# Layer 3's expert outputs: rows of X with bias and weight gathered by slot, sums scattered straight into the output

## The reference

```python
def _L3_ffn_ref(x, W1, b1, Wg, bg, Wd, bd):
    xf = x.reshape(-1, orig_shape[-1])                  # 625 x 256, layer-normed
    H = jax.nn.gelu(xf @ W1 + b1, approximate=False)    # 625 x 1024
    probs = jax.nn.softmax((H @ Wg + bg) / TEMP, axis=-1)
    assign = jnp.argmax(probs, axis=-1)
    out = jnp.zeros_like(xf)
    for e in range(Wd.shape[0]):                        # 8 experts
        y = H @ Wd[e] + bd[e]                           # 1024 -> 256
        sel = (assign == e)[:, None]
        out = out + jnp.where(sel, probs[:, e:e + 1] * y, 0.0)
    return out.reshape(orig_shape)
...
    x = x + _L3_ffn_ref(_layernorm(x, axis=-1)[None], ...)[0]
    return x
```

## Time and profile before

| what | us |
|---|---|
| median of three runs | 972.86 (970.52 to 976.18) |
| the profiled execution, its own time | 975.67 |
| its span, from first to last instruction | 973.5 |
| PE busy in the span | 892.7 (92%) |
| DVE busy | 447.8 (46%) |
| ACT busy | 281.1 (29%) |
| POOL busy | 182.1 (19%) |

### The profile page before, as it was taken

The page is one execution under the profiler, slowest core; times in us unless marked ns, Lnnn a source line. Parts: engine busy times, 40 slices in busy tenths (PEclk is TensorE's granted clock), DMA queues, the critical chain, the costliest instruction groups (busy, mean ns, idle before and its releaser), DMA issues.

```text
span 973.5 us, 15475 instructions
## 1 busy us (share of the span) xinstructions
PE 892.7 (92%) x5638; PEld 710.7 (73%) x5638; DVE 447.8 (46%) x1433; ACT 281.1 (29%) x625; POOL 182.1 (19%) x177
## 2 busy tenths in 40 slices
PE   6999998999999999999996778999999999899897
PEld 4776656889999877889875667777887554665665
DVE  7988555522222421632278976423434142340623
ACT  5111263122222114233347853332111111114210
POOL 2201000122221200045427751000101100000231
PEclk9999899999999999899988979999998899799899
DMA  8303001288885603159241000353100000320696
GB/s 296 142 2 92 1 1 38 96 303 315 320 325 192 235 1 130 54 187 322 98 164 68 1 1 1 130 192 120 45 1 14 19 1 1 130 96 35 206 344 230
DMA packets 28007, 120.42 MB, mean 124 GB/s; under 512 B 5401, under 2 KB 10032, under 8 KB 20132
## 3 DMA queue, kind: packets, MB, share of 16 engines
q1 hardware_dynamic: 22362, 104.39, 30.1%
q0 software_dynamic: 5280, 14.95, 4.6%
q10 hardware_dynamic: 295, 0.14, 0.1%
HBM read 106.11 MB, written 13.36 MB: 123 GB/s over the span
## 4 chain that ended last, share of the span: by engine, by line
PE 71%; DVE 15%; DMA 5%; issue 5%; ACT 2%; DVEq 1%; POOL 1%; SPq 0%; POOLq 0%; ACTq 0%
PE PS L817 8%; PE PS L473 6%; PE PS L441 5%; PE PS L832 5%; PE PS L884 4%; PE PS L868 4%; PE PS L485 4%; PE PS L552 4%; PE PS L627 2%; PE PS L908 2%; PE PS L959 2%; PE PS L948 2%; PE PS L1268 2%; DMA HT<-flat_rows,route 2%; DVE ring L1991 2%
## 5 line engine op out<-in xcount | busy, mean ns | idle before, releaser
L441 PE MATMUL PS<-const 128*128 128x128 f32 x674 | 92.8, 299 | 5.8 <-DVE X L1358 2.1
L441 PEld LDWEIGHTS PS<-const 128*128 128x128 f32 x674 | 88.2, 212 | 10.2 <-DVE X L1358 2.9
L817 PE MATMUL PS<-HT,ring 128*128 128x128 f32 x680 | 79.1, 275 | 3.3 <-DVE HT L1512 1.7
L817 PEld LDWEIGHTS PS<-HT,ring 128*128 128x128 f32 x680 | 78.4, 192 | 4.6 <-issue 3.9
L2655 POOL TENSOR_TENSOR col<-col,power 125x4 f32<-125x4 f32 (+2 forms) x13 | 11.9, 917 | 315.4 <-DVE col L1351 226.5
L2715 POOL DMA_INDIRECT slot_rows<-ST,route x41 | 41.4, 1010 | 151.1 <-ACT ST L2429 96.0
L2753 POOL TENSOR_TENSOR arena<-arena,ring 125x625 f32<-125x625 f32 x40 | 55.7, 1416 | 34.3 <-ACT arena L2517 30.1
L1911 DVE TENSOR_TENSOR HT<-HT,PS 128x256 f32<-128x256 f32 (+1 forms) x51 | 19.1, 376 | 89.8 <-ACT HT L2418 71.6
L627 PE MATMUL PS<-HT 125*128 125x126 bf16 x530 | 41.7, 230 | 6.8 <-DVE HT L1722 6.7
L1049 PE MATMUL PS<-w,HT 125*64 125x125 f32 x400 | 30.3, 305 | 18.0 <-DVE w L2010 18.0
L832 PE MATMUL PS<-ring,HT 128*128 128x256 f32 x204 | 46.8, 380 | 0.0
(11 more groups left out here) (472 smaller groups left out, 1712.3 us busy)
## 6 DMA issues: line engine op xcount, KB each, us to landing
ring<-in_experts SPq DMA_DIRECT2D x17, 1386.0 KB
ring<-in_experts SPq DMA_DIRECT2D x17, 768.0 KB, 6.0
ring<-in_experts SPq DMA_DIRECT2D x11, 1026.0 KB
arena<-in_experts SPq DMA_DIRECT2D x10, 1024.0 KB
ring<-in_experts SPq DMA_DIRECT2D x7, 1024.0 KB, 7.6
arena<-in_experts SPq DMA_DIRECT2D x6, 1026.0 KB
arena<-in_gnn SPq DMA_DIRECT2D x5, 1024.0 KB, 5.9
ring<-in_experts SPq DMA_DIRECT2D x8, 513.0 KB, 3.7
```

The source lines that it names most:

```text
L441: pe.matmul(PS[:, bank, 0:128], ident, ident, start=True, stop=True)
L817: mm = pe.matmul(PS[:, bank, at:at + SLOTS], both[:, j, k, m * 128:(m + 1) * 128], xs[0][i % 2][:, k, :], start=(k == 0), stop=(k == KD - 1))
```

## The change

Layer 3 no longer scatters to a cleared buffer, reads back and mixes. DVE writes the sum of X and the weighted bias rows to `X_weight` (257 columns a token, the last one the token's weight, with one more small copy), SP writes it to HBM as `weighted_rows` (640 KB, 1028 bytes a row), and POOL gathers those rows by slot as it gathers the hidden rows (`gather_start`, four ahead, nine in all). When a block's product is ready, DVE computes `PSUM * weight + row` in one operation (two for the last block), and POOL scatters the 128 rows (64 in the last block) into the output itself. Numbers of free slots lie over the bound of 624. Blocks 7 and 8 go the same way as the others, so the one-hot matrices and `add_late` fall away, and so do the read back, `mix_rows(3)`, the writes of X and the clearing in layer 0.

```diff
-SENT = {L: BLOCKS[L] - {3: 2}.get(L, 0) for L in PICKS}
@@ routing(L), DVE
+                row, less = dest_, float(pairs)
+                if L == 3:
+                    row, less = table[:, 0:blocks], 1.0
+                    link(dve.scalar_tensor_tensor(row, table[:, blocks:2 * blocks], float(TP), row, ALU.mult, ALU.add))
+                dve.scalar_tensor_tensor(to_row[:, 0:blocks], row, -less, empty_, ALU.add, ALU.add).then_inc(rows_ready, 1)
@@ layer0_moe(), DVE
-                dve.wait_ge(copy_out, 64)
@@ layer3_moe(), PE
-                for i in range(SENT[3], BLOCKS[3]):
-                    add_late(i)
@@ layer3_moe(), DVE
                 for t in range(NT):
                     b = bank()
-                    taken(dve.tensor_tensor(X[:, t, :], X[:, t, :], PS[0:TP, b, 0:D], ALU.add))
+                    taken(dve.tensor_tensor(X_weight[:, t, 0:D], X[:, t, :], PS[0:TP, b, 0:D], ALU.add))
                 own_banks()
-                token = CONST(const, "iota")[:, 0:N].rearrange("q (p t) -> q t p", t=NT)
-                for j in range(BLOCKS[3] - SENT[3]):
-                    dve.tensor_scalar(late_hot[j], token, float(NT), dest[:, SENT[3] + j:SENT[3] + j + 1], ALU.add,
-                                      ALU.is_equal).then_inc(picks_ready, 1)
+                dve.tensor_copy(X_weight[:, :, D:D + 1], mixes(3)).then_inc(layer_done, 1)
...
                         dve.wait_ge(ys_full, BASE[3] + i)
-                        if i > AHEAD[3]:
-                            dve.wait_ge(ys_out[b], rounds(3, i - 1 - AHEAD[3]))
-                        if i < BLOCKS[3]:
-                            dve.tensor_copy(ys[3][:, b, :], PS[:, 5 + (i - 1) % 2, 0:D]).then_inc(ys_taken, 1)
-                        else:
+                        dve.wait_ge(rows_moved[b], rounds(3, i - 1) - 16)
+                        parts = 64 if i == BLOCKS[3] else 128
+                        start = slot_start[0:parts, b, :]
+                        ins = dve.scalar_tensor_tensor(ys[3][0:parts, b, :], PS[0:parts, 5 + (i - 1) % 2, 0:D], start[:, D:D + 1],
+                                                       start[:, 0:D], ALU.mult, ALU.add)
+                        if i == BLOCKS[3]:
+                            link(ins)
                             dve.wait_ge(left_taken, BLOCKS[3] + 1)
-                            dve.tensor_tensor(ys[3][0:64, b, :], PS[0:64, 5 + (i - 1) % 2, 0:D], upper_half,
-                                              ALU.add).then_inc(ys_taken, 1)
-                mix_rows(3)
...
+                            ins = dve.scalar_tensor_tensor(ys[3][0:64, b, :], upper_half, start[:, D:D + 1], ys[3][0:64, b, :],
+                                                           ALU.mult, ALU.add)
+                        ins.then_inc(ys_taken, 1)
@@ exchange(L), POOL
             def scatter(L, i):
                 b = i % AHEAD[L]
                 pool.wait_ge(ys_taken, BASE[L] + i + 1)
+                if L == 3:
+                    parts = 64 if i == BLOCKS[3] - 1 else 128
+                    pool.indirect_dma_start(final, bass.IndirectOffsetOnAxis(to_row[0:parts, i:i + 1], 0),
+                                            ys[3][0:parts, b, :], None, bounds_check=N - 1,
+                                            oob_is_err=False).then_inc(rows_moved[b], 16)
+                    return
...
+            def gather_start(i):
+                b = i % AHEAD[3]
+                pool.indirect_dma_start(slot_start[:, b, :], None, weighted_rows,
+                                        bass.IndirectOffsetOnAxis(from_row[:, i:i + 1], 0),
+                                        bounds_check=N - 1, oob_is_err=False).then_inc(rows_moved[b], 16)
...
                 pool.wait_ge(rows_ready, 2 * NTH[L] + 2)
+                if L == 3:
+                    pool.wait_ge(copy_out, 64)
+                    for i in range(AHEAD[3]):
+                        gather_start(i)
                 for i in range(BLOCKS[L]):
                     if i + AHEAD[L] < BLOCKS[L]:
                         gather(L, i + AHEAD[L])
-                    if i < SENT[L]:
-                        scatter(L, i)
+                    scatter(L, i)
+                    if L == 3 and i + AHEAD[3] < BLOCKS[3]:
+                        gather_start(i + AHEAD[3])
@@ SP
-            sp.wait_ge(xn_ready, 2 * NT)
-            cleared = slot_rows[3][0:N, :].rearrange("(p t) d -> p t d", t=NT)
-            for p0, p1 in ((0, 120), (120, TP)):
-                sp.dma_start(cleared[p0:p1], nothing[p0:p1].unsqueeze(1).broadcast_to([p1 - p0, NT, D])).then_inc(copy_out, 16)
...
+            sp.wait_ge(layer_done, 1)
+            for p0, p1 in ((0, 120), (120, TP)):
+                sp.dma_start(weighted_rows.rearrange("(p t) d -> p t d", t=NT)[p0:p1], X_weight[p0:p1]).then_inc(copy_out, 16)
             sp.wait_ge(spill_ready, NTH[3] + 1)
...
-            rows_back(3)
-            for t in range(NT):
-                sp.wait_ge(layer_done, NT + t + 1)
-                sp.dma_start(out[0:120, t, :], X[0:120, t, :]).then_inc(out_done, 16)
-            sp.wait_ge(out_done, 160)
+            for b in range(AHEAD[3]):
+                sp.wait_ge(rows_moved[b], rounds(3, max(range(b, BLOCKS[3], AHEAD[3]))))
```

More of the change, by code:

```diff
@@ L66, in rounds @@
     b = i % AHEAD[L]
-    earlier = sum(len(range(b, SENT[M], AHEAD[M])) for M in PICKS if M < L and b < AHEAD[M])
-    return 16 * (earlier + i // AHEAD[L] + 1)
+    earlier = sum(len(range(b, BLOCKS[M], AHEAD[M])) for M in PICKS if M < L and b < AHEAD[M])
+    return 16 * (earlier + (2 if L == 3 else 1) * (i // AHEAD[L] + 1))
 def arrived(L, i):
@@ L350, in build @@
         mixed = {L: spare[0:TP, 0:2 * NT * D].rearrange("p (t k d) -> p t k d", t=NT, k=2) for L in (0, 1)}
-        mixed[3] = ROOT[:, :, :].unsqueeze(2)
         xs_rows = {0: view(spare, 2 * NT * D, 128, 4, D), 1: view(spare, 2 * NT * D, 128, 4, D),
@@ L375, in build @@
         second = where_rows[:, 2 * NT:3 * NT]
-        late_hot = [view(HT, 4 * HID3, 128, NT, TP), view(silu_flat, 0, 128, NT, TP)]
         upper_half = HT[0:64, 4 * HID3 + N:4 * HID3 + N + D]
-        late_sums = [PS[0:TP, b, 0:D] for b in (4, 7, 0, 1, 2)]
-        nothing = scratch[:, 0:D]
+        final = out.rearrange("p t d -> (t p) d")
+        X_weight = view(AT[:, :, :].rearrange("p t n -> p (t n)"), 0, TP, NT, D + 1)
+        weighted_rows = nc.dram_tensor("weighted_rows", [N, D + 1], F32).ap()
+        slot_start = view(w1, 0, 128, AHEAD[3], D + 1)
         hidden_turned = {}
@@ L1270, in down @@
                     mm.then_inc(ys_full, 1)
-                def add_late(i):
-                    first, last = i == SENT[3], i == BLOCKS[3] - 1
-                    pe.wait_ge(picks_ready, sum(PICKED.values()) + i - SENT[3] + 1)
-                    pe.wait_ge(ys_taken, BASE[3] + i + 1)
-                    for t in range(NT):
-                        mm = pe.matmul(late_sums[t], late_hot[i - SENT[3]][:, t, :], ys[3][:, i % AHEAD[3], :],
-                                       start=first, stop=last)
-                        if last:
-                            mm.then_inc(dve_full, 1)
-                            n["v"] += 1
                 stay_busy(0, 10)
@@ L1962, in layer1_moe @@
                         if i > AHEAD[1]:
-                            dve.wait_ge(ys_out[b], rounds(1, i - 1 - AHEAD[1]))
+                            dve.wait_ge(rows_moved[b], rounds(1, i - 1 - AHEAD[1]))
                         dve.tensor_copy(ys[1][:, b, :], PS[:, 5 + (i - 1) % 2, 0:D]).then_inc(ys_taken, 1)
@@ L2276, in last_rows_back @@
                 for b in range(AHEAD[L]):
-                    act.wait_ge(ys_out[b], rounds(L, max(range(b, SENT[L], AHEAD[L]))))
+                    act.wait_ge(rows_moved[b], rounds(L, max(range(b, BLOCKS[L], AHEAD[L]))))
                 back = slot_rows[L][0:PICKS[L] * N, :].rearrange("(p t k) d -> p t k d", t=NT, k=PICKS[L])
@@ L2427, in layer0_moe @@
                         if i > AHEAD[0]:
-                            act.wait_ge(ys_out[b], rounds(0, i - 1 - AHEAD[0]))
+                            act.wait_ge(rows_moved[b], rounds(0, i - 1 - AHEAD[0]))
                         act.activation(ys[0][:, b, :], PS[:, 5 + (i - 1) % 2, 0:D],
@@ L2627, in layer3_moe @@
                 act.activation(upper_half, PS[64:128, 5 + (BLOCKS[3] - 1) % 2, 0:D], ACT.Copy).then_inc(left_taken, 1)
-                last_rows_back(3)
-                for t in range(NT):
-                    act.wait_ge(layer_done, NT + t + 1)
-                    act.dma_start(out[120:TP, t, :], X[120:TP, t, :]).then_inc(out_done, 16)
             edges()
@@ L2758, in _ @@
             bias_to_x(ROWS3(rows3, "l3_ub2_0", TP), 8 * NT)
[L2759 removed]
+            pool.wait_ge(copy_out, 32)
             pool.wait_ge(index_ready, 1)
@@ L2863, in rows_back @@
                 for b in range(AHEAD[L]):
-                    sp.wait_ge(ys_out[b], rounds(L, max(range(b, SENT[L], AHEAD[L]))))
```

(1 more changed line is left out.)

30 lines of the change are left out of this document (7 added, 23 removed).

## The result

| | before | after |
|---|---|---|
| median, us | 971.7 (968.1 to 976.2) | 983.8 (980.8 to 985.3) |
| profiled execution, its own time | 975.67 | 985.25 |
| its span | 973.5 | 983.4 |

The changed kernel is slower: 1.0121 times the time before, 95% interval 1.0088 to 1.0154. The forecast was 977.2 and the range ended at 982.5; the median lies 1.3 us outside.

The account below looks back on a forecast made before the run. The prediction took PE to be held at the loop's end by gathers on a full software DMA queue. A loop loss of 8.7 us less a tail gain of 4.4 gave +4.3, so 977.2 us against 972.86, range 969 to 982.5.

Parts of the forecast that it names:

- What bounds the kernel: Layer 3's loop: PE runs at the pace of gathers on a full software DMA queue; a 9.0 us tail follows.
- The tail, removed, -4.4: After the last product: read back, mixing and writes of X go, so the end comes at 969.1 against 973.5.
- SP's last wait or the output's scatter is slow in another way: Rival at the kernel's end: the change does not do what it says; no size given, chance 0.03.
- Ahead of the loop: Before the loop: POOL waits for the written rows, gather_start 0 at 926.3, gather 4 at 931.5 instead of 921.66.
- A `gather_start` is 64 packets: In the loop: each gather of 1028-byte rows takes three rows a packet, 48 + 16 = 64 packets.
- The low bound: Loop's mildest case: 48 packets a gather_start, 16 fewer a scatter for free slots; loss 4.8, net +0.4 us.
- The rate, 35.4 packets a us: In the loop, 935 to 958: the speed at which the software queue q0 moves packets beside the weights.
- Gather 7 at 962.0, last product at 973.1, +8.7: End of the loop: queued packets land gather 7 at 962.0, not 953.04, and PE waits for it; loss 8.7 us.
- PE's clock falls: Rival in the loop: a lower PE clock from turn 7 on adds about 4 us, giving 981; chance 0.17.
- Small edits at nothing: Clearing, one-hot matrices, extra DVE operations and DVE's new wait cost nothing; under 1 us if uncovered.
- The queue has room: Rival in the loop: gathers land soon after issue, so the whole 4.4 us gain stays, 968.5; chance 0.2.

Follow-up runs that it names:

- e4: The changed kernel without the gathers of starting rows of blocks 4 to 8; ratio 1.0111 to the kernel before.
- e1: The kernel before plus one late 64-row gather by GpSimd after DVE's last mixed tile, which SyncE waits for; ratio 1.0047 to the kernel before.
- e2: The changed kernel without the last two scatters, of blocks 7 and 8; ratio 1.0022 to the kernel before.
- e3: The changed kernel with gathers 4 and 5 issued ahead of the wait for weighted_rows, nothing left out; ratio 1.0081 to the kernel before.
- e9: The kernel before with the gather of block 4 issued behind the scatter of block 0, nothing added; ratio 1.0032 to the kernel before.
- e7: The changed kernel with gathers 4 and 5 ahead of the wait for weighted_rows and each later gather ahead of the scatter; 974.8 us, ratio 1.0047 to before.
- e8: The changed kernel with gathers early as in e7 and without the starting rows of blocks 4 to 8 as in e4; 976.5 us, ratio 1.0048 to before.

## Why the prediction was wrong

Wrong was the tail, and with it the sum. Its own steps, in order:

- **What bounds the kernel**: right. PE is late for gathers, and it was the loop that lost most. Expected were waits of 2 to 4 us ahead of each of turns 4 to 7; turn 4 came 2.6 us late, turn 5 not at all, and turns 6, 7 and 8 waited 2.4, 1.0 and 0.9 us.
- **The tail, removed, -4.4**: this step failed. Its arithmetic held as far as it went: DVE's last operation ended at 973.56 and SP knew of the landing at 976.6, so 4.1 us from last product to landing where I had 4.6. But I followed only the data. With the write of X gone, nothing covers GpSimd's drain of 8.99 us, to which the prediction gave nothing: +6.5 us, and the tail's change is +1.8 instead of -4.4. The drain was in before's trace, 8147 ns from 958.8, and I never looked at it: I asked which work comes last and not what each engine still does when it has none left. "SP's last wait or the output's scatter is slow in another way" stood among the rivals at 0.03 and was not this.
- **Ahead of the loop**: nearly right. `gather_start` 0 at 927.91 for 926.3, gather 4 at 933.14 for 931.5; 0.9 us of each because the stage began at 914.92 and not 914.05.
- **A `gather_start` is 64 packets**: wrong, it is 48. The page's line for queue 0 before and after:

```profile
q0 software_dynamic: 5280, 14.95, 4.6%
```

```profile
q0 software_dynamic: 5792, 15.86, 4.7%
```

  512 more: nine of 48 and the two added scatters, of 48 and 16 + 16 packets. e4 shows it directly, with five `gather_start` fewer and 5552 packets, 240 fewer. The 16 packets on top of those with data are borne out by e1, whose gather of 64 rows added 80. That leaves 32 packets for 128 rows, so four rows of 1028 B, on average, did go in one packet. The Trainium skill, "DMA: Bandwidth & Descriptors", section "SWDGE vs HWDGE vs iDMA", puts a packet at 4096 B preferably. 4112 B went in one here, so the measurement decides against my reading of it. The low bound was also wrong in dropping 16 packets a scatter for the free slots: e2 leaves out the last two scatters and has 5712 packets, 80 fewer, which is their full count.
- **The rate, 35.4 packets a us**: low. In 935 to 958 after moved 958 packets of q0 and 809 of q1:

```profile
q1 hardware_dynamic: 809, 5.89, 65.8%
q0 software_dynamic: 958, 2.98, 33.8%
```

  41.7 a us for q0. The two together did 76.8 a us, against 74.6 before: the share moved, the sum hardly.
- **Gather 7 at 962.0, last product at 973.1, +8.7**: the numbers came out (turn 7 at 960.48, last product at 972.5, +8.1), the mechanism only in part. Gathers 6, 7 and 8 were each waited for, not gather 7 alone. The count of all packets gave the right size by luck: e4 takes 192 of them away and gains 0.4 us, and e3 takes none away and gains 5.0. What counts is when the gathers leave: gather 4 first of all (e3, e9), and the later ones too (e7 against e3, 36.9 for 38.1 us).
- **"PE's clock falls"**, 0.17: it did happen, in e4 (3.0 us behind one wait of 5.45) and for part of one product in after (953 to 957, behind a wait of 2.41; the step lost 1.7 us more than turn 7's own wait). Its place was a long wait in the middle of the loop, not turn 7 onward as I had it. In e9 a wait of 3.06 us left the clock up, so the waits alone don't tell when it falls.
- **Small edits at nothing**: right in after. Their margin was that VectorE's wait for the starting rows ends in time, and in e7 and e8, where those rows come later, it cost 0.7 and 2.0 us.
- **The queue has room**, 0.2: refuted by flights of 8.15 and 12.86 us in after. The Trainium skill, "DMA: Bandwidth & Descriptors", section "Anatomy of one DMA", fits 2.0 us plus bytes over 436 GB/s, an estimated 3.2 us for such a gather. The trace does not agree with it for this filled queue.

Ahead of the result the sum read 8.7 - 4.4 = 4.3; in the pair of traces it was 8.1 + 1.8 = 9.9.

## What to carry to other kernels

An engine's final drain is work like any other: look at each engine's last row before you shorten the tail, and let the engine with the long drain be done first. Where a new wait has to go into a queue of issues, put the issues that somebody waits for ahead of it; here that order alone was worth some 6 of the 10 us, with every added transfer still there. Then look at what came to stand behind them: here the starting rows of block 0, at 0.7 to 2.0 us. And a count of all the packets in a shared queue can give the right loss for the wrong reason. Leave some of them out to see, and read where the time went and not only the total: in e4 one wait went and another came.

## What the runs showed of the hardware that I had not expected

- GpSimd's final drain took 7.9 to 10.9 us. It grew by about 0.08 us with each indirect transfer that the program had issued (84: 8.15, 119: 10.93), and came also behind a memset (7.92).
- While GpSimd issued 24 indirect transfers without a pause, ScalarE waited up to 8.66 us at a time for signals of TensorE, 20.4 us in all, where 0.79 us at most is usual; with 1.85 us or more between twelve of them there was no such wait. Fourteen in a row in e2 did no harm.
- Four rows of 1028 B, on average, go in one packet of queue 0 (48 packets for 128 rows), as four of 1024 B do.
- An indirect scatter keeps its full count of packets when rows are out of bounds and skipped: the last two, of 128 and 64 rows of 1 KB, are 80 packets but only 0.07 MB (e2 against after, 15.79 and 15.86 MB).
- A gather of 524 KB issued into the stretch in which the weights load flew 8.15 to 12.86 us in after, 9.59 in e9 and 16.77 in e2.
